# Pieces of the exponentials begun two steps ahead, a sixth piece in units 0 to 15, and the channel groups' outputs summed by one reduction

## The chip, the cores and the metric

One core of a Trainium2 chip runs the whole program. The metric is the device time of one execution in microseconds (us); the time of a kernel is the median of several runs.

## The reference, cut to what matters

A transformer layer with 8 sequences (batches) of 512 positions and width 128, 16 heads of 8 dimensions. Attention is computed 16 times for each head, once for each "channel" w, with the same queries, keys and values and another factor on the scores, and the 16 outputs are added with weights:

```python
cos_pm = jnp.cos(phase_modulators)                    # (16 channels, 16 heads)
def wl_step(acc, wl):
    cpm, iw = wl
    scores = einsum('bhqd,bhkd->bhqk', Q*cpm, K*cpm) * SCALE
    scores = scores * cos(KERR * scores * scores)     # KERR = 2.7e-12
    attn = softmax(scores, axis=-1)
    return acc + einsum('bhqk,bhkd->bhqd', attn, V) * iw, None
acc, _ = lax.scan(wl_step, zeros, (cos_pm, interference_weights))
x = layernorm(x + (acc / 16) @ Wo + bo)
x = layernorm(x + feed_forward_with_experts(x))
```

So for each batch and head 512 x 512 scores are made once, and 16 x 512 x 512 exponentials of them are needed, each channel's with its own factor cos(pm)^2.

## The kernel before

A **unit** is one head of four batches: 32 units, units 0 to 15 for batches 0 to 3 and units 16 to 31 for batches 4 to 7. The scores of a unit stand transposed in the tile `s_t`: keys on the 128 partitions, and 8192 columns, that is 4 key tiles (kt) of 4 batches of 512 queries. There are two such buffers, one for the unit at work and one for the next.

The exponentials are shared by two engines. ACT (ScalarE) makes channels 0 to 14, one instruction each over the 8192 columns (L694), with the channel's factor as its scale; of channel 14 it leaves out some last columns (L691, `ACT_LAST`). DVE (VectorE) makes all of channel 15 and what is left of channel 14, in **pieces** of at most 2048 columns: piece n below 4 is key tile n of channel 15, piece 4 the rest of channel 14. That rest is set by `SHARED_B`: in units 0 to 15 the whole last key tile (2048 columns, ACT keeps 6144), in units 16 to 31 the last three batches of it (1536 columns, ACT keeps 6656). A piece is seven instructions, its **ops** 0 to 6 in `piece_dve`: op 0 scales and rounds to an int16, op 1 takes the fraction, op 2 builds a power of two, ops 3 to 6 are a polynomial. Each op but op 3 waits for the one ahead of it by a semaphore. The results stand in one of two buffers `x_p`, and op 3 of piece n+2 waits until PE has used piece n (`piece_used`).

PE (TensorE) multiplies each channel's exponentials by the values (L1392, and L800 for a piece). Three channels fill one PSUM bank (`W_GROUPS`, six groups a unit, the last of them channel 15 alone); a bank is copied out by DVE (`copy_products`, L1524), turned by PE (L1362), and normalized by DVE (`weigh`: a reciprocal L1534, a product L1538), which then adds the group to a running sum (L1544) and after the sixth group folds the three slots of that sum by two more additions (L1549, L1552).

A unit has 15 steps w = 0 to 14, one for each instruction of ACT. DVE and PE run an order written out by hand, step by step. In a step DVE has first the ops of pieces that a table names (`PIECE_STEPS`: step to a range of numbers i, where piece i // 7, op i % 7), then a copy, then a group's weighing, then its part of the next unit's preparation: projections (L906, step 1), row maxima (L911, steps 2 to 5), scores copied to `s_t` (L923, steps 8 to 11). PE has its part by `PRODUCT_STEPS`, `COPY_STEPS` and `TURN_STEPS`. In units 16 to 31 there are also steps of the feed-forward part for the batches finished before, whose small statistics are worked out by POOL (GpSimd; DVE then waits for it at L1006). Behind unit 31 stands the tail: the rest of the feed-forward part and the experts.

ACT's instruction for channel w waits for PE to have used the buffer of channel w-2 (`pv_done`) and, at a unit's start, for the scores (`st_copied`). Nothing else holds it.

Of the kernel before, what the change touches and what calls it, by code (L numbers as in the profile page):

```python
# [6 lines left out]
ALU = mybir.AluOpType  # L7
# [8 lines left out]
P = 128  # L16
# [26 lines left out]
SHARED_B = (0, 1)  # L43
ACT_LAST = [T * X_COLS - (NB - b) * S for b in SHARED_B]
PIECES = T + 1
# [3 lines left out]
LOWEST_Y = -126.0  # L49
EXP2_A, EXP2_B, EXP2_C, EXP2_D = 5.5933580, 42.364143, 197.45122, 12068.066  # L50
EXP2_ONE = 12068.069
# [15 lines left out]
GROUP_AT = [0, 1, 2, 3, 5, 4]
# [41 lines left out]
def postln_kernel(nc, a):  # L109
    with ExitStack() as ctx:  # L110
# [12 lines left out]
        weighted = sb("weighted", [P, SLOTS, GT * D])  # L123
        summed = sb("summed", [P, SLOTS, GT * D])
# [9 lines left out]
        x_2k = sb("x_2k", [P, X_COLS], BF16)  # L134
        x_n = x_2k[:].bitcast(I16)
# [8 lines left out]
        c2_head = sb("c2_head", [P, 1, W])  # L144
# [73 lines left out]
        gate_b = scratch(G + EXPERTS)  # L218
        assert taken[0] <= T * NB * S
# [8 lines left out]
        one_row = sb("one_row", [P, P])  # L228
# [279 lines left out]
        def _(pool):  # L508
# [3 lines left out]
            nc.gpsimd.memset(one_row[:], 1.0)  # L512
# [1115 lines left out]
```

## Time and profile before

| what | us |
|---|---|
| median of 3 runs | 3400.41 (3397.57 to 3402.31) |
| the profiled execution | 3401.9, span 3400.1 |
| ACT busy | 3316.0 |
| DVE busy | 3235.6 |
| PE busy | 2635.9, mean granted clock 0.942 of full speed |
| ACT's first channel instruction over 8192 columns starts at | 44.95 |
| ACT's last one of channel 14 starts at, and takes | 3314.45, 5.93 |

The span has a head of 45 us, 32 units, and a tail of about 80 us behind the last exponential.

### The profile page before, as it was taken

To read this page: it belongs to the slowest core of one execution; us is meant where nothing else is said; L and a number is where in the kernel's file an instruction comes from. 1 tells how busy PE (TensorE), PEld (TensorE's weight loads), DVE (VectorE), ACT (ScalarE), POOL (GpSimd) and SP (SyncE) were. 2 spreads that over 40 slices of the span, in tenths; PEclk is the share of its full clock that TensorE was granted. 3 is DMA by queue.
4 is the path that set the end of the run, shared out by engine and by line. 5 is a ranking of instruction groups with operands and counts; after the bars stand their busy time and mean duration, and the time that the engine had idled before them with its cause. 6 is when DMAs were issued, how large, how long until landed. Compare 5 with 4: busy or idle time off the path is not lost.

```text
span 3400.1 us, 47604 instructions
## 1 busy us (share of the span) xinstructions
PE 2635.9 (78%) x20641; PEld 755.2 (22%) x20641; DVE 3235.6 (95%) x2740; ACT 3316.0 (98%) x612; POOL 230.5 (7%) x321
## 2 busy tenths in 40 slices
PE   7777877777777777777777778788888777777776
PEld 2212222212221222221222222222222222222224
DVE  7999999999999999999999999999999999999997
ACT  7999999999999999999999999999999999999992
POOL 0000000000000000000001111101111101111000
PEclk8999899999999989999999999988999999999988
DMA  1000000000000000000000000000000000000001
GB/s 50 1 1 1 1 1 1 1 1 1 1 1 1 1 1 1 1 15 1 1 1 3 4 2 4 2 1 4 2 4 3 4 1 2 4 2 16 1 18 31
DMA packets 21400, 16.05 MB, mean 5 GB/s; under 512 B 4865, under 2 KB 19602, under 8 KB 20946
## 3 DMA queue, kind: packets, MB, share of 16 engines
q1 hardware_dynamic: 19922, 12.28, 1.2%
q8 instruction: 165, 2.70, 0.3%
q10 hardware_dynamic: 1152, 0.53, 0.1%
q0 software_dynamic: 128, 0.26, 0.0%
q14 instruction: 33, 0.27, 0.0%
HBM read 7.70 MB, written 5.37 MB: 4 GB/s over the span
## 4 chain that ended last, share of the span: by engine, by line
ACT 59%; issue 33%; ACTq 4%; DVE 2%; PE 2%; DMA 0%; POOL 0%; DVEq 0%
ACT probs L694 55%; ACTq L684 4%; ACT probs L691 3%; PE psum L1392 0%; ACTq L688 0%; DVE s_t L923 0%; DMA probs<-in_L_attn_bv_dram 0%; DVE m_pad L911 0%; DVE probs L976 0%; DVE probs L1006 0%; PE psum L950 0%; PE psum L945 0%; PE psum L1093 0%; PE psum L935 0%; PE psum L1112 0%
## 5 line engine op out<-in xcount | busy, mean ns | idle before, releaser
L694 ACT ACTIVATE probs<-s_t 128x8192 f32<-128x8192 f32 x447 | 3100.4, 7070 | 2.5 <-PE psum L1392 2.5
L1392 PE MATMUL psum<-probs,v_pad 128*27 128x512 f32 x15136 | 1889.3, 640 | 644.2 <-ACT probs L694 609.2
L1392 PEld LDWEIGHTS psum<-probs,v_pad 128*27 128x27 f32 x15136 | 458.4, 112 | 1990.1 <-issue 1007.6
L767 DVE SCALAR_TENSOR_TENSOR x_y<-s_t,c_last,x_2k 128x2048 f32<-128x2048 f32 (+1 forms) x160 | 369.5, 2310 | 2.4
L779 DVE SCALAR_TENSOR_TENSOR x_p<-x_p,x_y 128x2048 f32<-128x2048 f32 (+1 forms) x160 | 358.2, 2239 | 4.5
L787 DVE SCALAR_TENSOR_TENSOR x_p<-x_p,x_2k 128x2048 f32<-128x2048 f32 (+1 forms) x160 | 357.7, 2236 | 3.9
L783 DVE SCALAR_TENSOR_TENSOR x_p<-x_p 128x2048 f32<-128x2048 f32 (+1 forms) x160 | 357.2, 2232 | 2.4
L775 DVE SCALAR_TENSOR_TENSOR x_p<-x_y 128x2048 f32<-128x2048 f32 (+1 forms) x160 | 356.4, 2227 | 0.0
L923 DVE COPY s_t<-psum 128x2048 f32<-128x2048 f32 x128 | 292.1, 2283 | 8.7 <-PE psum L886 8.4
L911 DVE TENSOR_REDUCE m_pad<-psum 128x4 f32<-128x2048 f32 x128 | 292.4, 2286 | 5.9 <-PE psum L846 4.7
L764 DVE TENSOR_SCALAR x_2k<-s_t,c_last 128x2048 int16<-128x2048 f32 (+1 forms) x160 | 201.1, 1257 | 4.9 <-issue 1.0
L800 PE MATMUL psum<-x_p,v_pad 128*27 128x512 f32 x1248 | 181.4, 600 | 7.7 <-DVE x_p L787 7.4
L846 PE MATMUL psum<-qkv_t 8*128 8x512 f32 x1024 | 149.8, 656 | 46.4 <-DVE m_pad L911 37.8
L691 ACT ACTIVATE probs<-s_t,ln_one 128x6144 f32<-128x6144 f32 (+1 forms) x32 | 181.4, 5668 | 0.0
L886 PE MATMUL psum<-qkv_t 9*128 9x512 f32 x1024 | 148.2, 649 | 1.7 <-DVE s_t L923 1.6
L1524 DVE TENSOR_SCALAR o_sb<-psum,iw_col 128x512 f32<-128x512 f32 x192 | 142.7, 743 | 3.0 <-PE psum L1392 3.0
L521 POOL COPY w_head<-w_qkv 128x24 f32 (+1 forms) x31 | 32.4, 1046 | 1633.6 <-ACT probs L694 1621.7
L1362 PE MATMUL psum<-ident,o_sb 128*128 128x128 f32 x768 | 126.0, 287 | 9.6 <-DVE o_sb L1524 8.1
L532 POOL TENSOR_TENSOR loop_memory<-loop_memory 128x2 f32<-128x2 f32 x24 | 35.0, 1458 | 1380.3 <-DVE loop_memory L976 1380.3
L1534 DVE RECIPROCAL r_z<-psum 128x48 f32<-128x48 f32 (+1 forms) x192 | 79.9, 416 | 50.6 <-PE psum L1362 50.5
L1362 PEld LDWEIGHTS psum<-ident,o_sb 128*128 128x128 f32 x768 | 80.6, 141 | 174.8 <-issue 138.5
L771 DVE TENSOR_SCALAR x_2k<-x_2k 128x2048 int16<-128x2048 int16 (+1 forms) x160 | 111.9, 699 | 5.5
(251 smaller groups left out, 1080.8 us busy)
## 6 DMA issues: line engine op xcount, KB each, us to landing
s_t<-in_L_attn_x_dram SPq DMA_DIRECT2D x4, 256.0 KB, 7.2
x_next_dram<-x_p SPq DMA_DIRECT2D x1, 1024.0 KB, 4.5
x_group<-x_next_dram SPq DMA_DIRECT2D x1, 1024.0 KB, 4.8
loop_memory<-in_L_attn_x_dram SPq DMA_DIRECT2D x8, 128.0 KB, 2.1
x_dram<-loop_memory SPq DMA_DIRECT2D x8, 128.0 KB, 1.8
out_dram<-loop_memory SPq DMA_DIRECT2D x8, 128.0 KB, 1.8
x_dram<-probs SPq DMA_DIRECT2D x2, 512.0 KB, 4.8
out_dram<-probs SPq DMA_DIRECT2D x2, 512.0 KB, 4.0
```

The source lines that it names most:

```text
L691: nc.scalar.activation(probs[:, (p + w) % 2, 0:ACT_LAST[g]], s_t[:, p, 0:ACT_LAST[g]], ACT.Exp, bias=ln_one[:, 0:1], scale=scales[(p + w) ...
L694: nc.scalar.activation(probs[:, (p + w) % 2, :], s_t[:, p, :], ACT.Exp, scale=scales[(p + w) % 2]).then_inc(s["exp_done"], 1)
L764: nc.vector.tensor_scalar(at, scores, scale, LOWEST_Y, ALU.mult, ALU.max).then_inc(s["piece_chain"], 1)
L767: nc.vector.scalar_tensor_tensor(out=y, in0=scores, scalar=scale, in1=at, op0=ALU.mult, op1=ALU.subtract) \
L775: nc.vector.scalar_tensor_tensor(out=t, in0=y, scalar=EXP2_A, in1=y, op0=ALU.add, op1=ALU.mult) \
L779: nc.vector.scalar_tensor_tensor(out=t, in0=t, scalar=EXP2_B, in1=y, op0=ALU.add, op1=ALU.mult) \
L783: nc.vector.scalar_tensor_tensor(out=t, in0=t, scalar=EXP2_C, in1=t, op0=ALU.add, op1=ALU.mult) \
L787: nc.vector.scalar_tensor_tensor(out=t, in0=t, scalar=EXP2_D, in1=x_2k[:, 0:cols], op0=ALU.add, op1=ALU.mult) \
L911: nc.vector.tensor_reduce(m_pad[:, qt, :].rearrange("p (b l) -> p b l", l=L)[:, :, R_M:R_M + 1], banks(qt), AX.X, ALU.max, negate=True).th ...
L923: nc.vector.tensor_copy(s_t[:, p, kt * NB * S:(kt + 1) * NB * S], banks(kt).rearrange("p b q -> p (b q)")).then_inc(s["st_copied"], 1)
L1362: last = nc.tensor.transpose(psum[:, 6, qt * P:(qt + 1) * P], o_sb[:, at % 2, qt * P:(qt + 1) * P], ident[:])
L1392: last = nc.tensor.matmul(products_of(u, wg)[L * b:L * b + SLOTS * A, :], v_pad[:, p, b * T + kt, c0:c0 + SLOTS * A], probs[:, (p + w) % 2 ...
```

## The change

Three things are done. First, the ops 0 to 2 of a piece are written in another way: op 0 scales by 2^23 and rounds to an int32, so that op 1 (the fraction) and op 2 (the power of two) become bit operations on int32, both of the tensor_scalar kind. Second, the pieces are given more columns and other steps. ACT keeps 512 columns less of channel 14 in every unit: 5632 in units 0 to 15 and 6144 in units 16 to 31. Piece 4 is now the whole last key tile in all units, and units 0 to 15 have a sixth piece (n = 5) of 512 columns, the last batch of key tile 2. The tables name steps -2 and -1, which stand in the unit before, and PE's products of the pieces are moved likewise. Third, group 4 and 5 of a unit are no longer added to the running sum; they stay in their own slots of one tile `sums`, and one tensor_reduce over its seven slots gives the output.

```diff
-SHARED_B = (0, 1)
-ACT_LAST = [T * X_COLS - (NB - b) * S for b in SHARED_B]
-PIECES = T + 1
+SHARED_B = (3, 4)
+ACT_LAST = [(T - 1) * X_COLS - (NB - b) * S for b in SHARED_B]
+def pieces_of(u):
+    return T + 1 + (SHARED_B[u // H] < NB)
...
-PIECE_STEPS = {0: (0, 3), 1: (3, 5), 2: (5, 6), 3: (6, 8), 4: (8, 10), 5: (10, 12), 6: (12, 15), 7: (15, 18), 8: (18, 19),
...
-PRODUCT_STEPS = {6: 0, 8: 1, 11: 2, WA: 3, WA + 1: 4}
+FIVE_STEPS = {-2: (0, 3), -1: (3, 6), 0: (6, 10), 1: (10, 11), 2: (11, 12), 3: (12, 14), 4: (14, 16), 5: (16, 18), 6: (18, 21),
+SIX_STEPS = {-2: (0, 4), -1: (4, 7), 0: (7, 11), 1: (11, 12), 2: (12, 13), 3: (13, 16), 4: (16, 18), 5: (18, 20), 6: (20, 23),
+             7: (23, 26), 8: (26, 27), 9: (27, 31), 10: (31, 32), 11: (32, 34), 12: (34, 42)}
+FIVE_PRODUCTS = {3: 0, 6: 1, 9: 2, 12: 3, WA: 4}
+SIX_PRODUCTS = {3: 0, 6: 1, 9: 2, 12: 3, 14: 4, WA: 5}
...
             if op == 0:
+                if n == 0:
+                    dve.wait_ge(s["st_copied"], (u + 1) * T)
                 dve.wait_ge(s["piece_ready"], piece + 1)
                 nc.vector.tensor_scalar(at, scores, scale, LOWEST_Y, ALU.mult, ALU.max).then_inc(s["piece_chain"], 1)
             if op == 1:
                 dve.wait_ge(s["piece_chain"], base + 1)
-                nc.vector.scalar_tensor_tensor(out=y, in0=scores, scalar=scale, in1=at, op0=ALU.mult, op1=ALU.subtract) \
+                nc.vector.tensor_scalar(y.bitcast(I32), at, FRACTION_BITS, ONE_BITS, ALU.bitwise_and, ALU.bitwise_or) \
                     .then_inc(s["piece_chain"], 1)
             if op == 2:
                 dve.wait_ge(s["piece_chain"], base + 2)
-                nc.vector.tensor_scalar(at, at, 127.0, 128.0, ALU.add, ALU.mult)
+                nc.vector.tensor_scalar(at, at, EXPONENT_TOP, EXPONENT_BITS, ALU.bitwise_xor, ALU.bitwise_and)
...
-                    if at:
+                    if 0 < at < NWG - 2:
                         dve.wait_ge(s["norm_done"], n1 + 1)
-                        nc.vector.tensor_tensor(summed[:, 0:n, :], summed[:, 0:n, :], dst, ALU.add) \
-                            .then_inc(s["sum_done"], 1)
+                        nc.vector.tensor_tensor(summed, summed, dst, ALU.add).then_inc(s["sum_done"], 1)
...
-                        nc.vector.tensor_tensor(
+                        nc.vector.tensor_reduce(
                             comb[:, vg * GT:(vg + 1) * GT, h * D:(h + 1) * D].rearrange("p (b t) e -> p t b e", b=NB),
-                            weighted[:, 0, :].rearrange("p (t b d) -> p t b d", t=T, b=NB),
-                            summed[:, 2, :].rearrange("p (t b d) -> p t b d", t=T, b=NB), ALU.add) \
-                            .then_inc(s["comb_done"], 1)
+                            sums.rearrange("p r (t b d) -> p t b d r", t=T, b=NB), AX.X, ALU.add).then_inc(s["comb_done"], 1)
```

The order moves at three places that matter. At the start of unit 0 DVE has the ops below ahead of the next unit's projections (L906 before, L942 now). Before:

```order
L764 TENSOR_SCALAR x_2k<-s_t,c_last 128x2048
L767 SCALAR_TENSOR_TENSOR x_y<-s_t,c_last,x_2k 128x2048
L771 TENSOR_SCALAR x_2k<-x_2k 128x2048
L775 SCALAR_TENSOR_TENSOR x_p<-x_y 128x2048
L779 SCALAR_TENSOR_TENSOR x_p<-x_p,x_y 128x2048
L906 TENSOR_TENSOR qkv_t<-psum,b_head 128x1536
```

And now, on the same engine at the same place:

```order
L799 TENSOR_SCALAR x_i<-s_t,c_last 128x2048
L802 TENSOR_SCALAR x_y<-x_i 128x2048
L806 TENSOR_SCALAR x_i<-x_i 128x2048
L810 SCALAR_TENSOR_TENSOR x_p<-x_y 128x2048
L814 SCALAR_TENSOR_TENSOR x_p<-x_p,x_y 128x2048
L818 SCALAR_TENSOR_TENSOR x_p<-x_p 128x2048
L822 SCALAR_TENSOR_TENSOR x_p<-x_p,x_i 128x2048
L799 TENSOR_SCALAR x_i<-s_t,c_last 128x2048
L802 TENSOR_SCALAR x_y<-x_i 128x2048
L806 TENSOR_SCALAR x_i<-x_i 128x2048
L810 SCALAR_TENSOR_TENSOR x_p<-x_y 128x2048
L814 SCALAR_TENSOR_TENSOR x_p<-x_p,x_y 128x2048
```

Twelve ops stand there instead of five, since the ops of steps -2 and -1 have no unit before them. The second place is the end of a unit of the first half, steps 12 and 13, on DVE: the end of piece 4, the sixth piece in 512 columns, then the next unit's first ops.

```order
L822 SCALAR_TENSOR_TENSOR x_p<-x_p,x_i 128x2048
L799 TENSOR_SCALAR x_i<-s_t,c_last 128x512
L802 TENSOR_SCALAR x_y<-x_i 128x512
L806 TENSOR_SCALAR x_i<-x_i 128x512
L810 SCALAR_TENSOR_TENSOR x_p<-x_y 128x512
L814 SCALAR_TENSOR_TENSOR x_p<-x_p,x_y 128x512
L818 SCALAR_TENSOR_TENSOR x_p<-x_p 128x512
L822 SCALAR_TENSOR_TENSOR x_p<-x_p,x_i 128x512
L799 TENSOR_SCALAR x_i<-s_t,c_last 128x2048
L802 TENSOR_SCALAR x_y<-x_i 128x2048
L806 TENSOR_SCALAR x_i<-x_i 128x2048
L810 SCALAR_TENSOR_TENSOR x_p<-x_y 128x2048
```

Before, piece 4 ran through steps 13 and 14 to the unit's end and nothing of the next unit stood ahead of it. The third place is the last weighing of a unit, on DVE in step 2 of the next unit. Before:

```order
L1538 TENSOR_TENSOR weighted<-psum,r_z 128x16x3x8
L1544 TENSOR_TENSOR summed<-summed,weighted 128x384
L1549 TENSOR_TENSOR weighted<-summed 128x128
L1552 TENSOR_TENSOR comb<-weighted,summed 128x4x4x8
L911 TENSOR_REDUCE m_pad<-psum 128x4
```

Now:

```order
L1579 TENSOR_TENSOR sums<-psum,r_z 128x16x3x8
L1590 TENSOR_REDUCE comb<-sums 128x4x4x8
L947 TENSOR_REDUCE m_pad<-psum 128x4
```

One reduction that reads 7 x 128 elements, with a distance of 128 elements (512 bytes) from one to the next of a sum, stands for three additions, and a fourth, of 128 elements, is gone one step earlier.

## Rows read from the trace of the kernel before

**Rows 1.** The page: busy time, share of the span and instructions of each engine.
```profile
PE 2635.9 (78%) x20641; PEld 755.2 (22%) x20641; DVE 3235.6 (95%) x2740; ACT 3316.0 (98%) x612; POOL 230.5 (7%) x321
```

**Rows 2.** Timeline of ACT: start us, us, operation, idle before in brackets.
```profile
1158.45 5.44 ACT L691 ACTIVATE probs<-s_t,ln_one 128x6144 f32<-128x6144 f32 x1
1163.76 97.05 ACT L694 ACTIVATE probs<-s_t 128x8192 f32<-128x8192 f32 x14
1260.66 5.45 ACT L691 ACTIVATE probs<-s_t,ln_one 128x6144 f32<-128x6144 f32 x1
1267.37 97.03 ACT L694 ACTIVATE probs<-s_t 128x8192 f32<-128x8192 f32 x14 [1.26 <-PE psum L1392]
```

**Rows 3.** Groups by line and shape, ACT: count | busy us, mean ns.
```profile
L691 ACT ACTIVATE probs<-s_t,ln_one 128x6656 f32<-128x6656 f32 x16 | 94.6, 5913 | 0.0
L691 ACT ACTIVATE probs<-s_t,ln_one 128x6144 f32<-128x6144 f32 x16 | 86.8, 5422 | 0.0
```

**Rows 4.** Waits of DVE from 237 to 1773 us: us in total, times, longest.
```profile
DVE r_z L1534 <- PE psum L1362: 32.0, 19, 4.6
DVE s_t L923 <- PE psum L886: 4.8, 3, 2.3
```

**Rows 5.** Waits of DVE from 1773 to 3314 us.
```profile
DVE loop_memory L1006 <- POOL loop_memory L544: 26.9, 16, 1.8
DVE r_z L1534 <- PE psum L1362: 10.8, 8, 3.1
```

**Rows 6.** Timeline of DVE in unit 13, four successive rows, then two.
```profile
1366.89 1.29 DVE L764 TENSOR_SCALAR x_2k<-s_t,c_last 128x2048 int16<-128x2048 f32 x1
1368.21 2.35 DVE L767 SCALAR_TENSOR_TENSOR x_y<-s_t,c_last,x_2k 128x2048 f32<-128x2048 f32 x1
1370.60 0.69 DVE L771 TENSOR_SCALAR x_2k<-x_2k 128x2048 int16<-128x2048 int16 x1
1371.21 0.45 DVE L1534 RECIPROCAL r_z<-psum 128x48 f32<-128x48 f32 x1
...
1404.41 1.29 DVE L764 TENSOR_SCALAR x_2k<-s_t,c_last 128x2048 int16<-128x2048 f32 x1
1405.61 2.29 DVE L911 TENSOR_REDUCE m_pad<-psum 128x4 f32<-128x2048 f32 x1
```

**Rows 7.** Groups by line and shape, DVE: the pieces' operations.
```profile
L783 DVE SCALAR_TENSOR_TENSOR x_p<-x_p 128x2048 f32<-128x2048 f32 x144 | 329.1, 2285 | 1.9
...
L767 DVE SCALAR_TENSOR_TENSOR x_y<-s_t,c_last,x_2k 128x1536 f32<-128x1536 f32 x16 | 29.1, 1818 | 0.6
...
L783 DVE SCALAR_TENSOR_TENSOR x_p<-x_p 128x1536 f32<-128x1536 f32 x16 | 28.1, 1758 | 0.6
...
L764 DVE TENSOR_SCALAR x_2k<-s_t,c_last 128x1536 int16<-128x1536 f32 x16 | 16.3, 1019 | 0.5
```

**Rows 8.** The same view: the additions of the channel groups.
```profile
L1544 DVE TENSOR_TENSOR summed<-summed,weighted 128x384 f32<-128x384 f32 x128 | 71.6, 560 | 4.4
...
L1552 DVE TENSOR_TENSOR comb<-weighted,summed 128x128 f32<-128x128 f32 x32 | 9.4, 292 | 1.1
```

**Rows 9.** The same view: two reductions of 32 elements.
```profile
L1455 DVE TENSOR_REDUCE probs<-ident 128x8 f32<-128x32 f32 x1 | 0.2, 198 | 0.0
...
L1499 DVE TENSOR_REDUCE x_y<-x_y 128x1 f32<-128x32 f32 x1 | 0.2, 175 | 0.0
```

**Rows 10.** Timeline of POOL early in unit 21 and, below, late in it.
```profile
2196.46 1.72 POOL L536 TENSOR_TENSOR loop_memory<-loop_memory 128x2 f32<-128x2 f32 x1
...
2271.38 0.20 POOL L536 TENSOR_TENSOR loop_memory<-loop_memory 128x2 f32<-128x2 f32 x1
```

**Rows 11.** Timeline of PE at the end of unit 3.
```profile
441.76 6.38 PE L1392 MATMUL psum<-probs,v_pad 128*27 128x512 f32 x32 [3.29 <-ACT probs L694]
```

**Rows 12.** Timeline of DVE at the start of unit 0.
```profile
58.30 1.76 DVE L906 TENSOR_TENSOR qkv_t<-psum,b_head 128x1536 f32<-128x1536 f32 x1 [4.96 <-PE psum L829]
...
73.61 2.29 DVE L911 TENSOR_REDUCE m_pad<-psum 128x4 f32<-128x2048 f32 x1 [4.08 <-PE psum L846]
```

More of the change, by code:

```diff
@@ L42, with piece_no @@
 X_COLS = NB * S
-SHARED_B = (0, 1)
-ACT_LAST = [T * X_COLS - (NB - b) * S for b in SHARED_B]
-PIECES = T + 1
-LOG2_E = float(np.log2(np.e))
-LOWEST_Y = -126.0
-EXP2_A, EXP2_B, EXP2_C, EXP2_D = 5.5933580, 42.364143, 197.45122, 12068.066
-EXP2_ONE = 12068.069
+SHARED_B = (3, 4)
+ACT_LAST = [(T - 1) * X_COLS - (NB - b) * S for b in SHARED_B]
+def pieces_of(u):
+    return T + 1 + (SHARED_B[u // H] < NB)
+def piece_no(u, n):
+    return sum(pieces_of(v) for v in range(u)) + n
+LOG2_E = float(np.log2(np.e))
@@ L73, in steps_of @@
 def steps_of(u, usual, last):
-    return last if u == UNITS - 1 else usual
+    return last if u == UNITS - 1 else usual[u // H]
 def due(u, w, usual, last):
@@ L81, in due, with pieces_due @@
     return [(v, what) for v, what in now if what is not None]
+AHEAD = 2
+def pieces_due(u, w):
+    found = []
+    for v in (u, u + 1):
+        steps = steps_of(v, PIECE_STEPS, LAST_PIECE_STEPS) if v < UNITS else {}
+        at = w - (v - u) * WA
+        for step in range(-AHEAD if (u, v, w) == (0, 0, 0) else at, at + 1):
+            found += [(v, i) for i in range(*steps.get(step, (0, 0)))]
+    return found
 R_M = D
@@ L1389, in _ @@
                         for kt in range(T):
-                            for b in range(SHARED_B[g] if w == WA - 1 and kt == T - 1 else NB):
+                            for b in range(NB if w < WA - 1 or kt < T - 2 else SHARED_B[g] if kt == T - 2 else 0):
                                 at = (kt * NB + b) * S
@@ L1395, in _ @@
                                     start=(kt == 0 and w in FIRST_OF),
[L1396 removed]
+                                    stop=(w in LAST_OF and kt == T - 1) or (w == WA - 1 and kt == T - 2 and products_end_here(u)))
                         last.then_inc(s["pv_done"], 1)
@@ L1535, in weigh @@
                     dve.wait_ge(s["rz_done"], n1)
-                    dst = (weighted if at else summed)[:, 0:n, :]
-                    dve.wait_ge(s["sum_done"], v * NWG + max(at, 1))
+                    dst = (alone if n == 1 else weighted if at else summed)[:, 0:n, :]
+                    dve.wait_ge(s["sum_done"], v * ADDS + max(1, min(at, ADDS + 1)))
                     nc.vector.tensor_tensor(
```

76 lines of the change are left out of this document (42 added, 34 removed).

## The prediction

> **What bounds the kernel now.** I read the page first: ACT is busy for 98% of the span, DVE for 95%, PE for 78% [rows 1]. Two engines that full make an average useless, so I went to the timeline of ACT in the units. Its instructions stand end to end: in unit 11 fourteen of them start from 1163.76 to 1260.66, which is 96.90 / 14 = 6.92 us each, and the one of channel 14 takes 1163.76 - 1158.45 = 5.31 us from start to start [rows 2]. A unit is thus 14 x 6.92 + 5.31 = 102.2 us. ACT waits for PE in one place of the excerpt (1.26 us) and hardly anywhere else. ACT sets the end; every column taken from it shortens the span as long as nobody else is late.
>
> The second question is how much DVE can take. Its waits tell: in the 15 units from 237 to 1773 us (2 to 16, counted from one end of ACT's channel 14 to the next) it waits 36.8 us in all, 2.45 us a unit [rows 4]. In the 15 units behind them it waits 10.8 us for PE, only 0.72 us a unit; the other 26.9 us are for POOL [rows 5], and these don't shrink when DVE is late, because DVE itself starts POOL's chain with its statistics. They are no slack. So DVE is nearly as full as ACT, and most of all in units 16 to 31.
>
> **ACT's gain.** 512 columns less in each of 32 units. The two shapes of channel 14 differ by 512 columns and by 5913 - 5422 = 491 ns [rows 3]; between 6144 and 8192 columns it is (6.92 - 5.31) / 4 = 0.40 us [rows 2]. I take 0.43 between them: 32 x 0.43 = -13.8 us (-12.8 to -15.7).
>
> **What DVE pays for a piece.** From start to start op 0 takes 1.32 us, op 1 2.39, op 2 0.61 (nobody waits for it at once), and an operation of two inputs 2.285 + 0.03 = 2.32 [rows 6, 7]. A full piece is 1.32 + 2.39 + 0.61 + 4 x 2.32 = 13.6 us. The trace has no wide bit operation on int32. The bounds are op 0's price, the one-input operation on 4-byte data in the same buffers at about two elements a cycle (1.32, or 1.20 where the next doesn't wait for it [rows 6]), and one element a cycle as in L783 (2.32 and 2.21) [rows 7]. I take the first, as form and operands are op 0's and only the arithmetic differs. Op 1 then gives back 1.07, op 2 costs 0.59 more: -0.48 a full piece, 13.1 us.
>
> The Trainium skill, VectorE: DVE Perf Modes, the perf-mode tier table, gives tensor_scalar on fp32 in SBUF two elements a cycle, 1227 ns for 2048, and names no integer form. The sum by the page is the one above.
>
> Units 0 to 15: five full pieces, -2.4. The sixth piece, by the 2048 and 1536 shapes: the one-input ops lose 1.29 - 1.02 = 0.27 for 512 columns, so three of 0.48; the two-input ones lose 0.527, so four of 0.70 [rows 6, 7]; with the gaps 4.4 us. Units 16 to 31: four full pieces, -1.9; the fifth was 1.05 + 1.85 + 0.5 + 4 x 1.79 = 10.5 us [rows 7] (op 2 scaled from 0.61) and becomes 13.1: +2.6. Net +0.7.
>
> **The reduction.** Gone are an addition of 384 (0.56 + 0.03) and three of 128 elements (0.29 each) [rows 8]: 1.45 us. New is one of 896 elements. Dense, it would be 0.14 + 896 x 1.03 ns = 1.06 us (rate of the 512 columns above). But it reads at a distance of 512 bytes. The one reduction of the trace that reads at a distance, L1455, takes 198 ns for 32 elements where L1499 takes 175 [rows 9]: 0.72 ns more each, 1.71 us for 896. That pair is small, and part of the 23 ns may be its eight results in place of one. I take 1.4, and 1.06 and 1.71 as bounds: -0.35 to +0.3 a unit, 0 in the middle.
>
> The Trainium skill, Vector Engine (DVE) Microarchitecture Reference, the access granule in section 5.2, says that a source that hops 4 KiB at every element costs 1.73 ns each instead of 1.05. By it the reduction is an estimated 1.7 us, the upper bound; the pair in the trace agrees with it as far as 32 elements can, and its price is that of the first rival.
>
> **Is DVE in time?** Units 0 to 15: DVE +1.65 to +2.3, 2.0 in the middle, against 2.45 - 0.43 = 2.0 us of slack. It just fits; 0 to 0.3 us are missing in 15 units, 0 to 5 us, I take 0.5. Units 16 to 31: +0.35 to +1.0 against 0.72 - 0.43 = 0.29; 0.06 to 0.7 are missing, 1 to 11 us over 16 units. I take 0.25 a unit, 4 us, below the middle, since op 1 no longer reads two tiles while POOL works and L1006 keeps nearly the same filler: POOL's steps crawl behind DVE's (L536 1.72 us against 0.20 when left alone [rows 10]), and ahead of L1006 there are now three ops of 2.32 instead of four of 1.79 us.
>
> **The start.** Twelve ops now stand ahead of the projections: 13.1 + 1.32 + 1.32 + 1.20 + 2.32 + 2.21 = 21.5 us instead of 8.9 and a wait of 4.96 us [rows 12]. L942, which was L906, comes 21.5 - 13.9 = 7.6 us later (13.9 being 8.9 + 4.96). PE's row maxima queue behind it, and so in the end ACT's next unit and the products of steps 4 and 5. The wait of 4.08 us at the second L911 [rows 12] absorbs most; what is left is at most 3.5. I take 1.5 us once.
>
> **PE.** One matmul more or less changes nothing at 78%. But ACT can be late by PE: after idling 3.29 us PE took 6.38 us for channel 13's block instead of the usual 3.6 [rows 11], in a stretch whose granted clock fell; ACT then waited 1.2 us, as 0.15 + 6.38 = 6.5 is longer than its 5.31. Now its instruction there is 4.88 us, and each such case costs 1.65. There are two in the whole trace: +0.9; I take 1.
>
> **Sum.** -13.8 + 1.5 + 0.5 + 4 + 1 = -6.8 us. Tail and head are otherwise the same; the last reduction stands for three additions there too. Against the profiled execution's 3401.9 us this is 3395.1; the median of the runs is 1.5 us below it, so 3393.6. I say **3393.5**. The likeliest case's own range is 3387 to 3398.
>
> **Rivals.**
> *DVE takes over as the bound, by the reduction's full price.* At 1.7 us, 0.3 us are missing in units 0 to 15 (4.5 us) and 0.7 in units 16 to 31 (11 us): 15.5 us for my 4.5, so 11 us above my sum, 3404.5; halfway 3400. For it: waits for PE of only 0.72 us a unit in the second half, and L1455. Against it: so small a pair. Chance 0.22.
> *The bit operations run at one element a cycle.* Each full piece costs 2.0 us more (1.00 + 1.01), the sixth 0.5. DVE is then the bound throughout: 16 x 10.5 + 16 x 10 = 328 us, about 3720. This ends on the slower side; it decides from 0.25 us an op on. For it: no wide int32 bit operation in the trace; against it: op 0 and op 2 already take conversions and int16 at their fast rates. Chance 0.08.
> *PE is late at the units' ends.* The 1.65 us apply in every unit where channel 13's block falls into the low clock. In 8 units more than now the whole gain is gone; in 12 it is 3411. Against it: PE now has a piece's product in step 12, so it is idle for less than those 3.29 us ahead of that block. For it: where ACT's period shrinks to 4.88, nothing else of PE's fits in. Chance 0.09.
> The forecast has 0.61.
>
> **Chances.** A measurement of this kernel tells changes over 0.2%, 6.8 us, from none; that is 3393.6, on which my number stands. Of the forecast's 0.61 I give 0.46 to faster, since ACT's part may be kept in full, and 0.15 to no change. The first rival gives 0.16 to no change and 0.06 to slower, the second 0.08 to slower, the third 0.04 and 0.05. Together: faster 0.46, same 0.35, slower 0.19. The range 3386 to 3406 leaves out the second rival, the far end of the third and a little below.
>
> **What would show it.** ACT: the shape 128x5632 from start to start 4.88 us, 6144 5.31; its waits for PE below 12 us in all, mostly in units 16 to 31. DVE: L802 and L806 at 1.29 us; at 2.29 the second rival holds. L1590 at 1.4; at 1.7 the first. Waits of DVE for PE near zero in both halves; if some are left in units 16 to 31 while ACT waits, it isn't DVE's fill but its order. L942 first at about 66 us. I am wrong below 3388 if DVE has slack that its waits don't show, and above 3400 if its missing microseconds are as many as the upper bounds say.

## The result, and the profile after

The changed kernel takes **3415.56 us** (median of 5, 3415.33 to 3418.6); the kernel before, run beside it, took 3401.32. The ratio is 1.0049, 95% interval 1.0038 to 1.0059: slower by half a per cent, where 0.2% faster was forecast. The profiled execution has a span of 3413.5 us, 13.4 more than before.

Three words are used below. PE's **block** of a channel is its 32 matmuls on that channel's exponentials. A unit's time, or **period**, runs from one start of ACT's channel 14 to the next. The **first half** is units 0 to 15, the second half units 16 to 31.

I read the page first. Its busy row, that of [rows 1], then the groups by line and shape of ACT and DVE (count | busy us, mean ns):

```profile
PE 2654.6 (78%) x20641; PEld 771.6 (23%) x20641; DVE 3263.6 (96%) x2757; ACT 3306.0 (97%) x612; POOL 239.7 (7%) x320
```
```profile
L723 ACT ACTIVATE probs<-s_t,ln_one 128x5632 f32<-128x5632 f32 x16 | 79.7, 4982 | 0.0
```
```profile
L802 DVE TENSOR_SCALAR x_y<-x_i 128x2048 int32<-128x2048 int32 x160 | 199.4, 1246 | 5.5
L806 DVE TENSOR_SCALAR x_i<-x_i 128x2048 int32<-128x2048 int32 x160 | 195.7, 1223 | 3.4
...
L1590 DVE TENSOR_REDUCE comb<-sums 128x128 f32<-128x896 f32 x32 | 58.4, 1825 | 1.1
```

ACT's work is 10 us less, the bit operations run at the fast rate as I took it (1.25 and 1.22 us), and only the reduction (1.83) is dearer than its bounds. What grew is what ACT waits. Its waits from 237 to 1773 us, where it had 2.5 us in all before [rows 2], and from 1773 to 3315 us, where it had none (us in total, times, longest):

```profile
ACT probs L726 <- PE psum L1433: 7.5, 13, 0.6
```
```profile
ACT probs L726 <- PE psum L1433: 11.4, 9, 2.5
```

The starts of ACT's channel 14 tell where the 13.4 us are. The head is 2.2 us shorter: the first instruction over 8192 columns starts at 42.77 for 44.95. Unit 0 takes 4.2 us more (from the first instruction over 8192 columns to that of channel 14, 94.15 for 89.99), units 1 to 16 together 0.3 more (1638.52 for 1638.21), units 17 to 31 8.6 more (1549.88 for 1541.30), and what follows 2.5 more (88.2 for 85.65); 4.2 + 0.3 + 8.6 + 2.5 - 2.2 = 13.4. ACT's columns should have given 6.6 and 6.2 us in the two long stretches. There are three losses and a rest.

**Loss 1, the end of a unit in the first half.** The timeline of ACT, the place of [rows 2]:

```profile
1161.16 4.98 ACT L723 ACTIVATE probs<-s_t,ln_one 128x5632 f32<-128x5632 f32 x1
1166.72 97.03 ACT L726 ACTIVATE probs<-s_t 128x8192 f32<-128x8192 f32 x14 [0.58 <-PE psum L1433]
1263.64 5.00 ACT L723 ACTIVATE probs<-s_t,ln_one 128x5632 f32<-128x5632 f32 x1
1269.20 7.04 ACT L726 ACTIVATE probs<-s_t 128x8192 f32<-128x8192 f32 x1 [0.57 <-PE psum L1433]
```

1263.64 - 1161.16 = 102.48 us. 14 of units 1 to 16 take 102.46 to 102.54 us; units 5 and 13 have 101.78 and 101.80, which is 102.21 less the 0.42 us of the columns. And the timeline of PE there:

```profile
1256.88 3.64 PE L1433 MATMUL psum<-probs,v_pad 128*27 128x512 f32 x32 [1.22 <-ACT probs L726]
1263.80 5.33 PE L1433 MATMUL psum<-probs,v_pad 128*27 128x512 f32 x32 [3.29 <-ACT probs L726]
1269.07 0.66 PE L1399 MATMUL psum<-ident,o_sb 128*128 128x128 f32 x4
```

Channel 13's block takes 5.33 us and ends at 1269.1; ACT's next instruction needs it and starts at 1269.20. The stretches of PE's clock (us, busy by engine, then PEclk) for the block ahead and for this one:

```profile
1256.88:1260.50 3.62, 3.62 (x32) 0.91 (x32) 3.62 (x4) 3.62 (x1) 0.00 (x0) 1.00 0.00 0
...
1263.80:1267.90 4.10, 4.10 (x24) 1.11 (x28) 3.89 (x6) 4.10 (x1) 0.00 (x0) 0.58 0.00 0
```

2.4 GHz, then 3.29 us of idle time, then close to 1.2 GHz. The page TensorE: Matmul & The Clock Gate of the Trainium skill (Part 1) says that idleness lowers the clock to half; the trace agrees here, but not everywhere: before, the same 3.29 us stood ahead of 12 of the 16 blocks of channel 13 in the first half and only two of them ran slow [rows 11]; now it stands ahead of 14, and all 14 ran slow. A pause of this length permits the low clock, it doesn't bring it each time. The other blocks of channel 13, four before and two now, were quick: there channel 12's block had met the low clock, so it ended late and left a pause of 1.6 us. Before, at the end of unit 5:

```profile
640.61 5.33 PE L1392 MATMUL psum<-probs,v_pad 128*27 128x512 f32 x32 [2.21 <-ACT probs L694]
647.52 3.64 PE L1392 MATMUL psum<-probs,v_pad 128*27 128x512 f32 x32 [1.59 <-ACT probs L694]
```

The first of these is as slow as the blocks of loss 1, and costs nothing: ACT's instruction beside it, that of channel 13, takes 6.92 us, not 4.88.

**Loss 2, the start of a unit in the second half.** ACT waits 0.9 to 2.5 us in units 18, 22, 24, 26 and 28, and 0.6 us in units 23 and 27. The timelines of DVE and of PE at the start of unit 18:

```profile
1897.40 0.60 DVE L1042 TENSOR_SCALAR loop_memory<-loop_memory 128x128 f32<-128x128 f32 x2 [1.98 <-POOL loop_memory L576]
1897.92 2.29 DVE L822 SCALAR_TENSOR_TENSOR x_p<-x_p,x_i 128x2048 f32<-128x2048 f32 x1
1900.24 1.30 DVE L799 TENSOR_SCALAR x_i<-s_t,c_last 128x2048 int32<-128x2048 f32 x1
1901.58 1.64 DVE L802 TENSOR_SCALAR x_y<-x_i 128x2048 int32<-128x2048 int32 x1
1903.25 1.23 DVE L806 TENSOR_SCALAR x_i<-x_i 128x2048 int32<-128x2048 int32 x1
1904.39 0.74 DVE L1565 TENSOR_SCALAR o_sb<-psum,iw_col 128x512 f32<-128x512 f32 x1
```
```profile
1905.19 0.67 PE L1399 MATMUL psum<-ident,o_sb 128*128 128x128 f32 x4 [4.13 <-DVE o_sb L1565]
1905.79 4.40 PE L865 MATMUL psum<-x_group,w_head 128*32 128x512 f32 x24
1910.03 3.61 PE L1433 MATMUL psum<-probs,v_pad 128*27 128x512 f32 x32
```

PE stands still for 4.13 us because the turn of group 4 waits for DVE's copy L1565, and that copy stands behind four ops of step 0. Behind the turn come the projections, 4.40 us at the low clock instead of 2.78, and channel 2's block, which ACT waits for: it starts again at 1913.71 after 2.49 us. In DVE's row nothing looks late; it is PE that waits.

The second half lost 14.8 us: it is 8.6 longer, and the columns should have made it 6.2 shorter. The waits of loss 2 are 11.4 of them. Most of what is left is loss 1 at a smaller price: 11 of the 15 blocks of channel 13 ahead of units 17 to 31 took 5.33 us too, and next to ACT's 6144 columns (5.31 us) such a block adds 0.28 us to a unit (102.49 for 102.21 in the run without the sixth piece, below), 3.1 us in all.

**Loss 3, unit 0.** L942 starts at 63.58 us. PE idled 4.96 us for it and made all that stood behind it slowly, channel 3's block too; ACT waited 4.04:

```profile
65.38 2.09 PE L882 MATMUL psum<-qkv_t 8*128 8x512 f32 x8 [4.96 <-DVE qkv_t L942]
67.40 1.93 PE L836 MATMUL psum<-x_p,v_pad 128*27 128x512 f32 x8
69.10 5.42 PE L1433 MATMUL psum<-probs,v_pad 128*27 128x512 f32 x32
```

**The rest.** What stands behind the start of ACT's last instruction of channel 14 takes 2.5 us more. One group of PE's there has a mean of 910 ns a matmul, and 592 before, so it too ran mostly at the low clock:

```profile
L1148 PE MATMUL psum<-s_t,probs 128*128 128x512 f32 x8 | 5.9, 910 | 0.0
```

### The profile page after: what moved, and what is told of

Same layout as the page of the kernel before. It is cut to its first block, busy times and chain, and to the rows that moved or that the text cites. A ratio compares the mean times of both kernels' runs of the same rounds, so it can differ in the third digit from the quotient of the medians.

```text
span 3413.5 us, 47684 instructions
## 1 busy us (share of the span) xinstructions
PE 2654.6 (78%) x20641; PEld 771.6 (23%) x20641; DVE 3263.6 (96%) x2757; ACT 3306.0 (97%) x612; POOL 239.7 (7%) x320
## 4 chain that ended last, share of the span: by engine, by line
issue 50%; ACT 35%; PE 5%; POOL 4%; DVE 3%; ACTq 2%; DMA 0%; POOLq 0%; DVEq 0%
ACT probs L726 35%; PE psum L1433 3%; ACTq L716 2%; POOL loop_memory L566 1%; POOL loop_memory L564 1%; POOL loop_memory L568 1%; ACT probs L723 0%; POOL loop_memory L576 0%; POOL loop_memory L615 0%; DVE s_t L959 0%; ACTq L720 0%; POOL w_head L553 0%; PE psum L865 0%; DVE x_p L814 0%; DVE m_pad L947 0%
## 5 line engine op out<-in xcount | busy, mean ns | idle before, releaser
L1433 PE MATMUL psum<-probs,v_pad 128*27 128x512 f32 x15072 | 1908.3, 650 | 579.8 <-ACT probs L726 571.5
L1433 PEld LDWEIGHTS psum<-probs,v_pad 128*27 128x27 f32 x15072 | 473.3, 113 | 1906.1 <-issue 1051.0
L818 DVE SCALAR_TENSOR_TENSOR x_p<-x_p 128x2048 f32<-128x2048 f32 x176 | 377.3, 2144 | 4.1
L822 DVE SCALAR_TENSOR_TENSOR x_p<-x_p,x_i 128x2048 f32<-128x2048 f32 x176 | 377.3, 2144 | 3.3
L814 DVE SCALAR_TENSOR_TENSOR x_p<-x_p,x_y 128x2048 f32<-128x2048 f32 x176 | 376.8, 2141 | 2.4
L810 DVE SCALAR_TENSOR_TENSOR x_p<-x_y 128x2048 f32<-128x2048 f32 x176 | 376.1, 2137 | 2.9 <-PE psum L836 2.9
L799 DVE TENSOR_SCALAR x_i<-s_t,c_last 128x2048 int32<-128x2048 f32 x176 | 215.6, 1225 | 6.5 <-issue 1.3
L802 DVE TENSOR_SCALAR x_y<-x_i 128x2048 int32<-128x2048 int32 x176 | 206.2, 1172 | 6.1
L806 DVE TENSOR_SCALAR x_i<-x_i 128x2048 int32<-128x2048 int32 x176 | 202.5, 1150 | 3.9
L723 ACT ACTIVATE probs<-s_t,ln_one 128x5632 f32<-128x5632 f32 (+1 forms) x32 | 166.2, 5193 | 0.0
L1565 DVE TENSOR_SCALAR o_sb<-psum,iw_col 128x512 f32<-128x512 f32 x192 | 142.7, 743 | 1.4 <-PE psum L1433 1.4
L1579 DVE TENSOR_TENSOR sums<-psum,r_z 128x384 f32<-128x384 f32 (+1 forms) x192 | 98.5, 513 | 6.6
```

The source lines that it names most:

```text
L799: nc.vector.tensor_scalar(at, scores, scale, LOWEST_Y, ALU.mult, ALU.max).then_inc(s["piece_chain"], 1)
L802: nc.vector.tensor_scalar(y.bitcast(I32), at, FRACTION_BITS, ONE_BITS, ALU.bitwise_and, ALU.bitwise_or) \
L806: nc.vector.tensor_scalar(at, at, EXPONENT_TOP, EXPONENT_BITS, ALU.bitwise_xor, ALU.bitwise_and)
L810: nc.vector.scalar_tensor_tensor(out=t, in0=y, scalar=EXP2_A, in1=y, op0=ALU.add, op1=ALU.mult) \
L814: nc.vector.scalar_tensor_tensor(out=t, in0=t, scalar=EXP2_B, in1=y, op0=ALU.add, op1=ALU.mult) \
L818: nc.vector.scalar_tensor_tensor(out=t, in0=t, scalar=EXP2_C, in1=t, op0=ALU.add, op1=ALU.mult) \
```

## The experiments

Three theories go through them. **1**: the low clock at the ends of the first half's units. **2**: the copy's place in DVE's order. **3**: DVE simply has too much to do, the reduction above all, and the rest follows. After each expectation stand the median time and its ratio to the kernel before, run on the same chip, with its 95% interval; 1.0049 is the changed kernel's. The stretches and waits are those of one profiled execution each. Edits are cut to what matters.

**Filling the idle time ahead of channel 13's block.** The weights are the zero columns of `v_pad`, so zeros are added.

```diff
+                        if w == 13 and u < H:
+                            for i in range(10):
+                                b = i % NB
+                                nc.tensor.matmul(products_of(u, wg)[L * b:L * b + VPAD, :], v_pad[:, p, 0, 0:VPAD],
+                                                 s_t[:, p, b * S:(b + 1) * S], start=False, stop=False)
                         pe.wait_ge(s["exp_done"], u * WA + (w + 1))
```


> The changed kernel, with ten more matmuls of 18 zero columns of weights (they add zeros to the bank of channels 12 to 14) ahead of PE's wait for channel 13's exponentials, in units 0 to 15 only. They fill about 2.3 of the 3.29 us for which PE idles there. Theory 1 (PE falls to the low clock in that idle time, its block takes 5.33 us and ACT's 4.98 us instruction can't hide it, 0.70 us a unit): L1433's block of channel 13 takes 3.6 us in the first half, ACT's wait of 0.58 us goes, the unit's period falls from 102.48 to about 101.8, the time by 9 to 10 us to about 3406. Theory 3 (DVE is too full and the rest follows from it): PE's clock is not the cause, ACT's waits stay or move, the time stays within 2 us of 3415.

3411.9 us, 1.0038 (1.0025 to 1.0052). Every unit from 1 to 16 takes 101.8 us but one (103.36). The stretch is 1630.4 us instead of 1638.5: 8.1 less, as theory 1 says. The median fell only by 3.7 us, where I had given 9 to 10, and the profiled span by 6.4 (3407.1 for 3413.5), since the second half took 1.5 us more, with waits of loss 2 at other units. Loss 1 is thus the clock; and what is won in one stretch shifts all that follows against the clock.

**One op moved by a step.**
```diff
-FIVE_STEPS = {-2: (0, 3), -1: (3, 6), 0: (6, 10),
+FIVE_STEPS = {-2: (0, 3), -1: (3, 7), 0: (7, 10),
```


> The changed kernel, with op 6 of piece 0 moved from step 0 to step -1 in units 16 to 30 (one op of 2.3 us less ahead of the copy of group 4, which PE's turn and projections wait for). Theory 2 (in the second half ACT waits since the copy L1565 comes late at the unit's start, so that PE idles 4.1 us for it and then makes the projections in 4.40 us at the low clock): the waits of 1.7 to 2.5 us in units 18, 22, 26, 27 and 28 go, the time falls by 8 to 11 us to about 3405. Theory 3 (DVE as a whole has too much to do in these units): the op is only done at another place, DVE is as late as before, the time falls by less than 3 us.

3413.28 us, 1.0040 (1.0026 to 1.0053), with waits of 1.0 to 2.5 us in units 18, 22, 24, 26, 28 and 30. The experiment was badly built, not theory 2 refuted: the copy is the last of step 0, so an op moved from step 0 to step -1 still stands ahead of it. A table of steps is an order, not a time.

**The additions back, the reduction out** (L1585 and L1590 as before the change).
```diff
-                        nc.vector.tensor_reduce(comb[...], sums.rearrange("p r (t b d) -> p t b d r", t=T, b=NB), AX.X, ALU.add)
+                        nc.vector.tensor_tensor(weighted[:, 0, :], summed[:, 0, :], summed[:, 1, :], ALU.add)
+                        nc.vector.tensor_tensor(comb[...], weighted[:, 0, :], summed[:, 2, :], ALU.add)
```


> The changed kernel with the additions of before in place of the reduction over seven slots. DVE has 1.825 - 1.45 = 0.38 us less to do a unit. Theory 3 (DVE too full, the reduction's price decides): the second half gets 16 x 0.38 = 6 us or more faster, the first half nothing or up to 6 us, the time is 3404 to 3410. Theories 1 and 2: the first half stays (DVE waits 0.6 us a unit there and ACT's waits have another cause), the second gains a part of 6 us at most where the copy comes 0.38 us earlier; the time falls by 0 to 4 us.

3405.82 us, 1.0017 (1.0008 to 1.0026): 0.32% less, as theory 3 had it. The first half is as long as with the reduction (1638.5, with 14 units at 102.46 to 102.52), the second 6.7 us shorter, with waits of 0.9 to 1.7 us in units 18, 20, 24 and 26 only. Here 0.4 us a unit less for DVE decides how often PE comes late; theory 3 seems to hold for the second half.

**No sixth piece.**
```diff
-SHARED_B = (3, 4)
+SHARED_B = (4, 4)
```


> The changed kernel without the sixth piece: ACT makes 6144 columns of channel 14 in units 0 to 15 as before (16 x 0.43 = 7 us more) and DVE has 4.4 us less to do a unit. Theory 1 (low clock at the units' ends): a block of 5.33 us nearly hides under an instruction of 5.4 us, the period is 102.21 to 102.4 instead of 102.48, so the time falls by 1 to 4 us although ACT has more to do. Theory 3 (DVE too full in the first half too): likewise no more than these 4 us, but then the wait of 0.58 us goes because DVE comes earlier, and the blocks of 5.33 us are gone too.

3412.3 us, 1.0039 (1.0025 to 1.0053). The sharpest evidence for loss 1: ACT has 512 columns more and DVE 4.4 us less in each unit, and 14 of units 1 to 16 still take 102.45 to 102.52 us. PE's blocks of channel 13 ran slow there too, now hidden but for 0.28 us. Unit 0 lost nothing (90.0 us, as before): by the table of five pieces eleven ops stand ahead of L942 and not twelve, PE's pause for it is 2.65 us and not 4.96, and the three groups behind it took 1.14, 1.06 and 3.62 us, the full clock's times. The second half, whose code is unchanged, took 6 us more: how many of its units lose depends on where the clock's low stretches fall.

**The fifth piece of the second half back at 1536 columns.**
```diff
+EXTRA_B = (0, 1)
-ACT_LAST = [(T - 1) * X_COLS - (NB - b) * S for b in SHARED_B]
+ACT_LAST = [(T - 1) * X_COLS - (NB - b) * S + e * S for b, e in zip(SHARED_B, EXTRA_B)]
```


> The changed kernel with the fifth piece of units 16 to 31 at 1536 columns and ACT at 6656 there, as before. DVE has 2.6 us less to do in each of these units, ACT 0.43 us more. Theory 3 (in the second half DVE has about 0.3 us a unit more to do than time): ACT's waits there (11.4 us) go, its 7 us come back, the second half takes 1541 to 1545 us instead of 1550, the time falls by 5 to 9 us. If the copy's place in the order is the cause and not the amount: the waits stay at 8 us or more and the time rises by about 4 us.

3408.97 us, 1.0021 (1.0012 to 1.0030). ACT waits in one unit of the second half only (21, twice, 1.47 us in all), as theory 3 says, and DVE waits 48 us for PE; so the 2.6 us were more than enough. Unit 0, whose order and work are those of the changed kernel, took 92.7 us for its 94.15: behind the same pause for L943 (4.99 us) channel 3's block took 3.95 us and not 5.42. Loss 3 too depends on where the low clock ends.

**Filling PE's idle time ahead of the turn**, eight matmuls by zero weights in step 1 of units 17 to 31:
```diff
+                        if w == 1 and u > H:
+                            for i in range(8): ...
                         for v, at in due(u, w, TURN_STEPS, LAST_TURN_STEPS):
                             turn_products(v, at)
```


> The changed kernel, with eight more matmuls by zero weights ahead of PE's turn of group 4 in step 1, in units 17 to 31 only. They fill 1.8 of the up to 4.1 us for which PE waits for DVE's copy L1565 there. Theory 2b (that wait drops PE's clock, and the projections L865 behind it take 4.40 instead of 2.78 us, which makes most of ACT's wait): L865 takes 2.8 us in all units, ACT's waits in the second half fall from 11.4 us to below 5, the time by 5 to 8 us. Theory 3 (the copy comes late since DVE is too full, and that alone makes the wait): PE is as late as DVE is, the waits shrink by less than 3 us.

3408.04 us, 1.0023 (1.0014 to 1.0032), with waits of 2.5, 2.0 and 0.55 us left in units 18, 24 and 30, 5.2 us in all, and 1543.7 us for units 17 to 31: the low clock makes a good part of loss 2. The copy still comes late, and in units 18 and 24, where PE still paused for 2.43 and 1.94 us behind the filling, the projections took 4.32 and 4.44 us.

**Three at once**: the additions, the filling ahead of channel 13's block, and a table for unit 0.
```diff
+FIRST_STEPS = {0: (0, 5), 1: (5, 7), 2: (7, 10), 3: (10, 14), 4: (14, 18), 5: (18, 20), 6: (20, 23), 7: (23, 26),
+               8: (26, 27), 9: (27, 31), 10: (31, 32), 11: (32, 34), 12: (34, 42)}
```


> The changed kernel with three edits together: the additions in place of the reduction, the matmuls by zero weights ahead of channel 13's block in units 0 to 15, and in unit 0 a table of its own, by which DVE has 5, 2, 3, 4 and 4 ops in steps 0 to 4 and not 11, 1, 1, 3 and 2. If the three losses are separate (the reduction in the second half, the clock at the ends of units 0 to 15, the start), they add: 9.5 + 9 + 4 = 22 us less than 3415.6, about 3393. If the units' phase against the clock decides how many waits there are, less comes: with 3400 or more the losses weren't separate.

3401.25 us, 1.0000 (0.9991 to 1.0009). Less than the sum, which was 3393: channel 13's blocks were quick, but from unit 6 to 14 the projections ran slow, and ACT waited 0.4 us a unit at the other end. With the copy late there was no margin there.
```profile
774.09 0.66 PE L1404 MATMUL psum<-ident,o_sb 128*128 128x128 f32 x4 [1.97 <-DVE o_sb L1575]
774.67 4.48 PE L870 MATMUL psum<-x_group,w_head 128*32 128x512 f32 x24
```

**ACT's columns undone** (the two edits of `SHARED_B` and `EXTRA_B` together), the rest of the change kept.

> The changed kernel with ACT's columns of before (6144 and 6656, no sixth piece, the fifth with 1536 columns in the second half); the rewritten ops, the earlier steps and the reduction stay. Theory 1 (PE's low-clock block sets the end of a unit in the first half): units 1 to 16 still take 102.49 us as with 5632 columns, and the second half, where DVE now has 2.6 us less to do, has no waits: 102.65 and 102.85 us as before; the time is 3403 to 3406, slower than before although DVE has less to do in every unit. Theory 3 (all of the loss is DVE's fill): both halves are as before, 3397 to 3401.

3408.62 us, 1.0024 (1.0014 to 1.0033). Units 1 to 16 take 102.2 to 102.5, 14 of them over 102.45, the second half 1544.3 us with waits in two units. So theory 3 is wrong for the first half: with less to do for DVE and the same for ACT than before, the unit's end is still PE's. The time is 3 us above what I gave; the stretch behind the last channel 14, 90.6 us here for 85.65, has them.

**The reduction alone, in the kernel before.**

> The kernel before with the one reduction in place of the additions, nothing else. DVE has 0.38 us more to do a unit; it waits for PE 2.45 us a unit in the first half and 0.72 in the second. If these waits are slack, nothing comes of it: 3399 to 3402. If DVE's waits in the second half aren't slack for the copy at the unit's start, up to 0.38 x 16 = 6 us and a few slow projections on top: 3405 to 3410.

3401.95 us, 1.0004 (0.9995 to 1.0013). It takes 1.81 us there and costs nothing: nearly all periods are those of before. (In units 0 to 13 channel 13's block has pauses of 0.3 to 1.9 us ahead of it, so this run says little on loss 1.) The reduction is no loss by itself; it became one where the copy had no margin.

**The copy of group 4 ahead of the ops of step 0.** The same work, another order.
```diff
+                        if w == 0:
+                            for v, at in due(u, w, COPY_STEPS, LAST_COPY_STEPS):
+                                copy_products(v, at)
                         for v, i in pieces_due(u, w):
                             piece_dve(dve, i // PIECE_OPS, i % PIECE_OPS, v, v % 2, v % H)
-                        for v, at in due(u, w, COPY_STEPS, LAST_COPY_STEPS):
-                            copy_products(v, at)
+                        if w:
+                            for v, at in due(u, w, COPY_STEPS, LAST_COPY_STEPS):
+                                copy_products(v, at)
```


> The changed kernel, with DVE's copy of group 4 ahead of the pieces' ops in step 0 instead of behind them: the same work, the copy some 6 us earlier against DVE's own row. (The earlier run that moved op 6 from step 0 to step -1 left the copy behind the same ops, so it didn't test this.) Theory 2 (place of the copy): PE's wait for it at the turn L1399 goes, the projections start 2 to 4 us earlier, ACT's waits in units 18 to 30 (11.4 us) fall below 3, the first one in unit 0 (4.0) stays, the first half stays at 102.48; the time falls by 8 to 11 us to 3404 to 3408. Theory 3 (amount of DVE's work): DVE is as late as before with all that follows, other waits take their place, the time falls by less than 3 us.

3399.54 us, 0.9997 (0.9988 to 1.0006), 16 us less than the changed kernel. Units 17 to 31 take 1536.8 us instead of 1549.9; ACT's waits there fall from 11.4 to 0.3 us; units 1 to 16 lose what they lost (1637.8 us, 13 of them at 102.47 to 102.56). It is 4 us below the 3404 I gave; the stretch behind the last channel 14 has 3.6 of them (84.6 us for 88.2). The timelines of DVE and PE at the start of unit 18:
```profile
1895.79 0.60 DVE L1042 TENSOR_SCALAR loop_memory<-loop_memory 128x128 f32<-128x128 f32 x2 [1.98 <-POOL loop_memory L576]
1896.31 0.74 DVE L1565 TENSOR_SCALAR o_sb<-psum,iw_col 128x512 f32<-128x512 f32 x1
1896.97 2.28 DVE L822 SCALAR_TENSOR_TENSOR x_p<-x_p,x_i 128x2048 f32<-128x2048 f32 x1
```
```profile
1896.32 3.64 PE L1433 MATMUL psum<-probs,v_pad 128*27 128x512 f32 x32 [3.29 <-ACT probs L726]
1899.89 0.66 PE L1399 MATMUL psum<-ident,o_sb 128*128 128x128 f32 x4
1900.48 2.78 PE L865 MATMUL psum<-x_group,w_head 128*32 128x512 f32 x24
```
The turn follows the block at once, the projections run at 2.4 GHz. DVE does as much as before, the reduction included: theory 2, and DVE's amount of work only decides how much too late a badly placed copy comes.

**The copy and the filling.** 

> The same, and the matmuls by zero weights ahead of channel 13's block in units 0 to 15. If the two losses are separate they add: 8 us more, 3396 to 3400, which is at or a little below the kernel before.

**3389.18 us** (3388.68 to 3394.26), 0.9969 (0.9957 to 0.9981): 0.3% faster than the kernel before, and below the 3396 I gave. Units 1 to 16 take 101.8 us each, all 16, and no unit of the second half has a wait of loss 2. The filling (L1428) and channel 13's block (L1439, which was L1433) at the end of unit 11:
```profile
1255.19 2.75 PE L1428 MATMUL psum<-s_t,v_pad 128*18 128x512 f32 x20
1258.67 3.64 PE L1439 MATMUL psum<-probs,v_pad 128*27 128x512 f32 x32 [0.74 <-ACT probs L727]
```

**And the additions and the table of unit 0.** 

> The same, and the additions of before in place of the reduction, and unit 0's own table: 0.38 us less for DVE a unit and 4 us at the start. 3388 to 3394 if every loss found so far is mended, about 3400 if PE's low clock only moves to another block, as it did with the three edits without the copy.

3390.93 us, 0.9970 (0.9959 to 0.9982): no better. Unit 0 gained 2.8 us, a wait of 1.41 us for PE in unit 17 took half of it back; the reduction costs nothing any more.

**The same two mends in the kernel before.** 

> The kernel before, with the two edits that made the changed one faster: the copy of group 4 ahead of the pieces' ops in step 0, and ten matmuls by zero weights ahead of channel 13's block in units 0 to 15. If the change itself gives the 13.8 us of ACT's columns once its two losses are mended, this kernel gains only the two waits of 1.2 and 1.3 us that it had in the first half: 3397 to 3400. If the mends alone make the gain (they would help any version), it comes near 3389.

3400.02 us, 0.9998 (0.9988 to 1.0007). So the 0.3% are the change's own; the mends are worth nothing without it.

**Piece 3's product in the idle time, in place of zeros**, with the copy ahead.
```diff
-SIX_PRODUCTS = {3: 0, 6: 1, 9: 2, 12: 3, 14: 4, WA: 5}
+SIX_PRODUCTS = {3: 0, 6: 1, 9: 2, 13: 3, 14: 4, WA: 5}
```


> The changed kernel with the copy of group 4 ahead of the pieces' ops, and in units 0 to 15 piece 3's product in step 13 instead of 12: PE has it (1.06 us) in the idle time ahead of channel 13's block and not ahead of channel 12's. If it is the length of that idle time (3.29 us, then 2.3) that brings the low clock, the block takes 3.6 us and the time is as with the matmuls by zero weights, 3388 to 3392. If 1 us of work in it is too little, the period stays at 102.48 and the time at 3399.

3392.6 us, 0.9977 (0.9968 to 0.9986), between the two answers. Units 1 to 5 take 101.8 us, units 6 to 16 102.4: the block is slow there although the pause ahead of it is 2.43 us. Behind the same pause ahead of units 3 and 4 it was quick (3.64 us).
```profile
1258.06 1.04 PE L836 MATMUL psum<-x_p,v_pad 128*27 128x512 f32 x8
1261.54 5.22 PE L1433 MATMUL psum<-probs,v_pad 128*27 128x512 f32 x32 [2.43 <-ACT probs L726]
```

**The reduction by itself**: ten of them near the start of the changed kernel, run once (3434.15 us; the time isn't what was asked). L1484 has its seven elements side by side, L1485 64 bytes apart, L1487 512.


> The changed kernel with ten more reductions of 7 x 128 elements near its start, whose results go nowhere: twice each with 4, 64, 256 and 512 bytes from one element of a sum to the next, and the kernel's own form. If the distance sets the price (the first rival's reading of the pair of 32 elements), the dense one takes 1.06 us and the one at 512 bytes 1.8. If it is the 128 results or the form of the operand, the dense one takes 1.8 too.


```profile
12.01 1.08 DVE L1484 TENSOR_REDUCE x_y<-sums 128x128 f32<-128x896 f32 x1
13.00 1.65 DVE L1485 TENSOR_REDUCE x_y<-sums 128x128 f32<-128x896 f32 x1
...
16.13 1.65 DVE L1487 TENSOR_REDUCE x_y<-sums 128x128 f32<-128x896 f32 x1
17.70 1.65 DVE L1488 TENSOR_REDUCE x_y<-sums 128x128 f32<-128x896 f32 x1
```
Dense, 0.99 us from start to start; apart, 1.57 whatever the distance between 64 and 512 bytes, and the kernel's own form the same 1.65 us.

## Why the prediction was wrong

- **ACT's columns**: right. 102.21 - 101.80 = 0.41 us a unit in the first half for 0.43. In the second half the mended kernel's units are 0.3 to 0.4 shorter than before.
- **The pieces' ops**: right, 1.26 and about 1.2 us from start to start; the second rival is out.
- **The reduction**: 1.4 was too low and the upper bound of 1.71 too, it takes 1.83 us. The pair of 32 elements pointed the right way; the lower bound was that of a dense operand, which this isn't. Of the 1.83, 1.65 are its form; what adds 0.18 in the units isn't settled (ACT and PE are at work there, and its results go to other places).
- **Is DVE in time?** This is the first of the two steps that failed, and the larger, by 9 us and more. I set DVE's added work of a unit against its waits for PE in that unit, as if slack were one number. It isn't: what counts is when PE gets the copy of group 4. I had shown the new order of ops for the starts of unit 0 and of steps 12 and 13, but not asked what the ops of step 0 do to the copy behind them. The 4 us for the second half were 13 by the experiment with the copy moved (1549.9 - 1536.8; four slow blocks of channel 13 fewer are 1.1 of them). The 0.5 us for the first half were none: DVE waited 17.8 us for PE there, 1.2 a unit. My own sign for this case was in the trace: DVE waited 12.9 us for PE in units 17 to 31 while ACT waited 11.4, so it wasn't DVE's fill but its order. The first rival has the same symptom with the wrong cause: with the additions back the time is 3405.8, with the copy moved 3399.5 and the reduction kept.
- **PE**: this is the second step that failed, by 6 us: 14 x 0.7 = 9.8, less the 2.8 that the two long periods cost before (103.53 and 103.65 for 102.21), is 7 for my 1. The third rival's mechanism was right where I gave it 0.09. I counted the two slow blocks of before and took their number as fixed; there were 14. Its price was too high, 0.7 us each and not 1.65, since the block takes 5.33 us and not 6.38. I had also summed it wrongly: at 1.65 us four more units, and not eight, use up the 6.8 us that I forecast. Against it I had argued that PE's new product in step 12 shortens the idle time ahead of the block. It doesn't: the product is done ahead of channel 12's block, and 3.29 us stay 3.29.
- **The start**: 1.5 was taken with 3.5 as the most; 4.0 came. L942 starts at 63.6 and not at 66, but only because the head was 2.2 us shorter; from the first instruction over 8192 columns it is 7.5 us later than before, for my 7.6. PE's pause for it brought the low clock, and 2.09 + 1.93 + 5.42 us took the place of 1.14 + 1.06 + 3.62, 3.6 us more. I had priced the wait and not the clock behind it.
- **Sum**: 7 us for my 1 at the ends of the first half's units, 14.8 for my 4 in the second half, 4.2 for my 1.5 at the start and none for my 0.5 are 19 us above the 3395.1 that I had for the profiled execution, which took 3415.3, 20 more. That so little is left is partly luck: the head and the end, of which I had said that they stay the same, moved by -2.2 and +2.5 us. With the two mends, the time is 3389 and the forecast's reason holds.

**What stays open**: why the low clock falls on channel 13's block in nearly every unit after the change and seldom before, with the same 3.29 us of idle time ahead. Not that PE runs at it: before, one to five blocks of every unit of the first half were slow too (4.9 to 6.6 us for 3.64), mostly those of other channels, where ACT's longer instruction hid it. It is neither the columns (undone, it stays), nor the reduction (with the additions back, it stays), nor the copy's place (moved, it stays); the rewritten ops and the steps of PE's and DVE's row are left, and weren't tried one by one. Nor is it shown that the 2.5 us behind the last channel 14 are the change's: that stretch took 82.5 to 90.8 us in the profiled executions of the experiments, and 90.8 with the reduction alone in the kernel before, for 85.65 and 88.2.

## What to carry to other kernels

When ops are moved ahead in an engine's order, look at what stands behind them and who waits for it, not at the engine's total: one copy put ahead of four ops was worth 13 us in units 17 to 31 and 16 us in the median, with the same work. Give TensorE's clock a price at each pause that a change leaves or makes: it costs nothing where the block has room, and more than the gain where ACT's instruction beside it has become shorter than the slow block (0.7 us for 0.42 here). And when a change comes out slower, test its parts with the order mended before it is thrown away; the parts were worth 0.3%.

## What the hardware showed that I had not expected

- The low clock comes back at the same block unit after unit, and leaves it after some. Before, the two long periods of the first half are units 4 and 12; after, the two short ones are units 5 and 13. The eight units between them are no rule: the short ones are seven apart in four experiments (units 6 and 13 with the additions back) and three in two. The mean granted clock is no measure of harm: 0.942 before, 0.932 after, and 0.916 in the fastest kernel.
- PE ran at the low clock behind a pause of 2.43 us, and at the full one behind one of 3.29 (the block of 1896.32 us above); with the filling, behind pauses of 0.74 us and less, no block of channel 13 was slow in the first half of the fastest kernel.
- A reduction whose elements aren't side by side takes 1.57 us for 896 elements at 64 bytes apart as at 512, 0.58 more than a dense one. The Vector Engine (DVE) Microarchitecture Reference of the Trainium skill (the access granule in section 5.2) gives 1.73 ns an element for a source that hops 4 KiB every element. By this case's runs, 1.57 us / 896 = 1.75 ns an element stands already at 64 bytes.
